# Inverting the 16x16 diagonal blocks of a head's triangular matrices on VectorE, gathered and scattered by DMA, with K and Q interleaved

## The reference, cut to what matters

```python
def step(state, inp):
    q_t, k_t, v_t, b_t, d_t = inp
    Sk = jnp.einsum('bhi,bhipj->bhpj', k_t, state)
    delta = (v_t - Sk) * b_t[..., None]
    upd = jnp.einsum('bhi,bhpj->bhipj', k_t, delta)
    state = state * d_t[:, :, None, :, None] + upd
    o = jnp.einsum('bhi,bhipj->bhpj', q_t, state)
    return (state, o)
```

## Time and profile before

| what | us |
|---|---|
| median of 3 runs | 1288.95 (1286.04 to 1291.09) |
| the profiled execution | 1287.92 |
| its span, first to last instruction | 1286.2 |
| PE busy | 1232.8 (96%) |
| DVE busy | 1069.8 (83%) |
| ACT busy | 912.1 (71%) |
| POOL busy | 910.0 (71%) |

### The profile page before, as it was taken

One profiled execution on the slowest core, in us unless ns is written; L12 is line 12 of the kernel. 1 busy time (PEld: TensorE's weight loads), 2 busy tenths in 40 slices (PEclk: granted clock), 3 DMA queues, 4 the chain that ended last, 5 costly groups with the idle time before them and its releaser, 6 DMA issues.

```text
span 1286.2 us, 33400 instructions
## 1 busy us (share of the span) xinstructions
PE 1232.8 (96%) x12362; PEld 1059.9 (82%) x12362; DVE 1069.8 (83%) x2393; ACT 912.1 (71%) x2536; POOL 910.0 (71%) x1184
## 2 busy tenths in 40 slices
PE   9899988989999999999999999999999999999997
PEld 7565445778989898889998989989999889999885
DVE  5797225999888999998997897889898879888788
ACT  4003553587888778787878787778878878778675
POOL 3122443667887868867876878788888888878765
PEclk9898989999999999999999999999999999999999
DMA  7931112222111011210112212121321213121221
GB/s 232 242 104 38 45 40 95 83 46 75 29 46 45 26 35 42 67 35 24 45 37 69 62 51 79 45 85 51 84 54 48 83 34 88 31 83 30 74 69 54
DMA packets 62773, 83.77 MB, mean 65 GB/s; under 512 B 8276, under 2 KB 46420, under 8 KB 62612
## 3 DMA queue, kind: packets, MB, share of 16 engines
q1 hardware_dynamic: 57876, 67.34, 18.8%
q0 software_dynamic: 4736, 14.29, 4.0%
HBM read 68.65 MB, written 12.77 MB: 63 GB/s over the span
## 4 chain that ended last, share of the span: by engine, by line
PE 71%; DVE 17%; DMA 4%; issue 4%; ACT 3%; POOL 2%; SPq 0%; DVEq 0%; POOLq 0%; ACTq 0%
PE ps L1225 19%; PE ps L1622 4%; PE ps L1575 4%; PE ps L1589 4%; PE ps L1559 3%; PE ps L1518 3%; PE ps L1531 3%; PE ps L1528 3%; PE ps L1560 3%; PE ps L1585 3%; DVE yv L2003 2%; PE ps L1630 2%; PE ps L1412 2%; PE ps L1498 2%; PE ps L1597 2%
## 5 line engine op out<-in xcount | busy, mean ns | idle before, releaser
L2385 ACT ACTIVATE XY<-ps 128x512 f16<-128x512 f32 x384 | 218.2, 601 | 87.8 <-PE ps L1531 85.8
L2116 DVE TENSOR_TENSOR ZL<-ps,cst 128x256 f16<-128x256 f32 x384 | 151.9, 417 | 16.0 <-PE ps L1518 14.7
L2003 DVE SCALAR_TENSOR_TENSOR yv<-ps,cw,yv 128x511 f32<-128x511 f32 (+2 forms) x192 | 142.6, 744 | 6.6 <-ACT yv L2329 4.1
L1225 PE MATMUL ps<-XH,WVh 128*128 128x256 f32 (+1 forms) x384 | 131.8, 343 | 2.1 <-DVE xt L2201 1.4
L1225 PE MATMUL ps<-XH,WVl 128*128 128x256 f32 (+1 forms) x384 | 122.4, 319 | 0.0
L1225 PE MATMUL ps<-XL,WVh 128*128 128x256 f32 (+1 forms) x384 | 122.3, 319 | 0.0
L1528 PE MATMUL ps<-ZL,XY 128*128 128x64 f16 x1536 | 103.8, 193 | 1.5 <-DVE ZL L2116 1.2
L1531 PE MATMUL ps<-XY,ZL 128*128 128x64 f16 x1536 | 103.4, 193 | 0.0
L1518 PE MATMUL ps<-XY,LT 128*128 128x64 f16 x1536 | 93.8, 193 | 3.9 <-ACT XY L2385 2.7
L2419 ACT ACTIVATE sq<-O 128x128 bf16<-128x128 f32 x256 | 79.7, 311 | 19.6 <-DVE O L2166 8.3
L1518 PEld LDWEIGHTS ps<-XY,LT 128*128 128x128 f16 x1536 | 74.9, 98 | 22.0 <-issue 11.5
(11 more groups left out here) (337 smaller groups left out, 4279.3 us busy)
## 6 DMA issues: line engine op xcount, KB each, us to landing
RC<-crow SPq DMA_DIRECT2D x128, 128.0 KB
WV<-in_WV SPq DMA_DIRECT2D x16, 512.0 KB, 3.7
exr<-in_ex SPq DMA_DIRECT2D x16, 384.0 KB, 3.5
WK<-in_WK SPq DMA_DIRECT2D x16, 256.0 KB, 3.0
WO<-in_WO SPq DMA_DIRECT2D x16, 256.0 KB, 2.7
rows_out<-st SPq DMA_DIRECT2D x7, 512.0 KB
KS<-spread SPq DMA_DIRECT2D x12, 256.0 KB, 8.7
QS<-spread SPq DMA_DIRECT2D x12, 256.0 KB, 12.5
```

What stands on the lines that cost most here:

```text
L1225: m = pe.matmul(o, a, b, start=c + k == 0, stop=c == 1 and k == 2)
L2003: m = dve.scalar_tensor_tensor(out=dst[:, k:512], in0=ps[:, bk, 0:512 - k], scalar=cw[:, h, j, 3 - k:4 - k], in1=dst[:, k:512], op0=ALU.mu ...
L2116: leave(dve.tensor_tensor(half(ZL[:, k - 2], k, 0), p, lv(k), ALU.mult), "a", u, k)
L2385: leave(act.activation(changed(u, k), ps[:, bank("b", u, k), :].rearrange("p (c n t) -> p c n t", c=2, t=1 << (k - 1)), ACT.Copy), "b", u, k)
```

## The change

The levels 1 to 4 of every inverse are no longer done by `x1`, `a` and `b` on PE, DVE and ACT; `LEVELS` becomes `range(5, 8)`. In their place the 16x16 diagonal blocks are inverted directly:

- `gram`, `pl`, `pm` of a chunk come earlier (`plan_chunk`, rank `4 * h - 6.3 + 0.6 * i`). The two 16-bit parts of L go by DMA (`ls`) to an array `parked` in DRAM, and PT goes to `decayed` (`ps`).
- When the 4 chunks of a head are parked, 8 DMAs (`dg`) gather its 128 diagonal blocks (16 matrices x 8 blocks) into LC, one block of 256 elements to a partition. The run that a packet moves is 16 elements of 2 bytes.
- 16 DVE instructions (`iv1`, `iv2`, `iv3`) invert the blocks by substitution on sizes 2, 4, 8 and 16; each waits for the one before, save for the second ones of pairs.
- ACT casts the result and its transpose (`xc`), and 16 DMAs (`sx`) scatter them into the zeroed diagonal form in `parked`, again in runs of 32 bytes.
- For each chunk one DMA (`ld`) brings X, Y, L and the low part back into XYLM, and one (`pd`) brings PT back.
- Two DMAs write zeros to `parked` among the small loads of layer 0.
- K and Q share a tile KQ, and `gram` is one matmul of 256 columns to each sequence in place of two of 128.
- POOL's `py` and `xi` go; `pl` and `pm` do the same cast, subtraction and diagonal in another order.
- The keys of a head come earlier (rank `4 * h - 8.5` in place of `4 * h - 6`), and `RANK` and `LATER` have other numbers throughout, so that the order within all queues differs.

```diff
-LEVELS = range(2, 8)
-C_IO = C_LV + 6 * 64
+C_ID, C_SEL, C_U, C_ONE, C_LV = 0, 128, 256, 384, 512
+LEVELS = range(5, 8)
...
-    P.add(("pt", u), rank + 0.1, ("DVE", 0.79, (("gram", u), "DVE"), earlier(4, "so", "PE", 0), earlier(4, "so", "PE", 1)),
-          gives=("gram", u))
-    P.add(("pl", u), rank + 0.1, ("POOL", 1.5, (("gram", u), "DVE"), earlier(3, "c", "DVE"), earlier(3, "r", "PE")))
-    P.add(("py", u), rank + 0.1, ("POOL", 1.2, (("pl", u), "POOL")))
-    P.add(("pm", u), rank + 0.2, ("POOL", 1.2, (("pl", u), "POOL")))
-    P.add(("xi", u), rank + 0.1, ("POOL", 0.48, earlier(3, "r", "PE"), (("cc", 1), "POOL")))
-    P.add(("x1", u), rank + 0.4, ("PE", 0.12, (("pl", u), "POOL"), (("cc", 1), "POOL")),
-          ("DVE", 0.34, earlier(3, "r", "PE"), (("xi", u), "POOL")), takes=True, gives=("x1", u))
-    last = ("x1", u), "DVE"
+    P.add(("pt", u), rank + 0.1, ("DVE", 0.79, (("gram", u), "DVE"), earlier(2, "ps", "SP")), gives=("gram", u))
+    P.add(("ps", u), rank + 0.2, ("SP", 1.0, (("pt", u), "DVE"), earlier(8, "pd", "SP")))
+    P.add(("pl", u), rank + 0.1, ("POOL", 0.6, (("gram", u), "DVE"), earlier(2, "ls", "SP")))
+    P.add(("pm", u), rank + 0.1, ("POOL", 2.1, (("pl", u), "POOL")))
+    P.add(("ls", u), rank + 0.2, ("SP", 1.0, (("pm", u), "POOL"), earlier(8, "ld", "SP")))
+
+
+def plan_blocks(P, h):
+    rank = 4 * h - 3.8
+    units = [(("ls", 4 * h + i), "SP") for i in range(4)]
+    P.add(("dg", h), rank, ("SP", 4.0, *units, (("iv1", h - 1), "DVE") if h else None))
+    P.add(("iv1", h), rank + 0.1, ("DVE", 2.5, (("dg", h), "SP"), (("xc", h - 1), "ACT") if h else None))
+    P.add(("iv2", h), rank + 0.1, ("DVE", 1.3, (("iv1", h), "DVE")))
+    P.add(("iv3", h), rank + 0.1, ("DVE", 1.3, (("iv2", h), "DVE")))
+    P.add(("xc", h), rank + 0.2, ("ACT", 0.9, (("iv3", h), "DVE"), (("sx", h - 1), "SP") if h else None))
+    P.add(("sx", h), rank + 0.2, ("SP", 8.0, (("xc", h), "ACT")))
...
+    P.add(("ld", u), rank - 0.5, ("SP", 1.5, (("sx", h), "SP"), earlier(3, "c", "DVE")))
+    P.add(("pd", u), rank + 0.5, ("SP", 1.0, (("ps", u), "SP"), earlier(2, "so", "PE", 0), earlier(2, "so", "PE", 1)))
+    last = ("ld", u), "SP"
...
+        parked = nc.dram_tensor("parked", (2, 4, 128, 16, 128), F16, kind="Internal").ap()
+        decayed = nc.dram_tensor("decayed", (8, 128, 512), F32, kind="Internal").ap()
...
+        KQ = sb("KQ", [128, 3, 2, 1024])
+        K, QC = KQ[:, :, 0, :], KQ[:, :, 1, :]
...
+                for k in range(2):
+                    sp.dma_start(parked[k, 0:2].rearrange("k p q t -> k p (q t)").bitcast(U16),
+                                 A["blank"].unsqueeze(0).broadcast_to((2, 128, 2048))).then_inc(d_l1, 16)
...
+                elif what == "ps":
+                    w.wait_ge(*done("gram", h))
+                    if h > 7:
+                        w.wait_ge(d_pd[h % 2], 16 * ((h - 8) // 2 + 1))
+                    sp.dma_start(decayed[h % 8], PTE[:, h % 2].rearrange("p l t -> p (l t)")).then_inc(d_ps[h % 2], 16)
+                elif what == "ls":
+                    w.wait_ge(s_one, nth("POOL", "pm", h))
+                    if h > 7:
+                        w.wait_ge(d_ld[(h - 8) % 3], 16 * ((h - 8) // 3 + 1))
+                    i = 4 * (h % 4)
+                    sp.dma_start(parked[h // 4 % 2, 2:4, :, i:i + 4, :].rearrange("k p q t -> p k (q t)"), LM[:, h % 2]
+                                 ).then_inc(d_ls[h % 2], 16)
+                elif what == "dg":
+                    for p in range(2):
+                        w.wait_ge(d_ls[p], 16 * (2 * h + 2))
+                    if h:
+                        w.wait_ge(s_iv, IV * (h - 1) + 1)
+                    for b in range(8):
+                        at = slice(16 * b, 16 * b + 16)
+                        sp.dma_start(LC[at].rearrange("q (j i) -> q j i", i=16),
+                                     parked[h % 2, 2, at, :, at].rearrange("j q i -> q j i")).then_inc(d_dg, 16)
+                elif what == "sx":
+                    w.wait_ge(d_l1, 96)
+                    w.wait_ge(s_xc, 2 * h + 2)
+                    for b in range(8):
+                        at = slice(16 * b, 16 * b + 16)
+                        for k in range(2):
+                            sp.dma_start(parked[h % 2, k, at, :, at].rearrange("r q c -> q r c"),
+                                         XY16[at, k, :].rearrange("q (r c) -> q r c", c=16)).then_inc(d_sx, 16)
+                elif what == "ld":
+                    w.wait_ge(d_sx, 256 * (h // 4 + 1))
+                    if h > 2:
+                        w.wait_ge(*done("c", h - 3))
+                    i = 4 * (h % 4)
+                    sp.dma_start(XYLM[:, h % 3], parked[h // 4 % 2, :, :, i:i + 4, :].rearrange("k p q t -> p k (q t)")
+                                 ).then_inc(d_ld[h % 3], 16)
+                elif what == "pd":
+                    w.wait_ge(d_ps[h % 2], 16 * (h // 2 + 1))
+                    if h > 1:
+                        for b in range(2):
+                            w.wait_ge(*full("so", h - 2, b))
+                    sp.dma_start(PT[:, h % 2].rearrange("p l t -> p (l t)"), decayed[h % 8]).then_inc(d_pd[h % 2], 16)
...
-                        kt = K[:, h % 3, 128 * n:128 * n + 128]
-                        pe.matmul(ps[:, bk, 256 * b:256 * b + 128], kt, kt, start=True, stop=True)
-                        m = pe.matmul(ps[:, bk, 256 * b + 128:256 * b + 256], kt,
-                                      QC[:, h % 3, 128 * n:128 * n + 128], start=True, stop=True)
-                    signal(m, *x)
-                elif what == "x1":
-                    u = x[1]
-                    bk = enter(*x)
-                    w.wait_ge(s_const, 2)
-                    w.wait_ge(s_lt, nth("POOL", "pl", u))
-                    for l in range(4):
-                        m = pe.matmul(ps[:, bk, 64 * l:64 * l + 64], LT[:, u % 3, l, :], half(id16[:], 1, 0), start=True, stop=True)
+                        at = slice(128 * n, 128 * n + 128)
+                        m = pe.matmul(ps[:, bk, 256 * b:256 * b + 256].rearrange("p (k t) -> p k t", k=2),
+                                      K[:, h % 3, at], KQ[:, h % 3, :, at], start=True, stop=True)
...
+            def times_left(wd, o, to):
+
+                left = part_of(XC, 17 * o + 16 * wd, (16, wd), (0, wd), (1, wd))
+                upper = part_of(XC, 17 * o, (0, wd), (1, wd), (16, wd))
+                dve.tensor_tensor(to.rearrange("p (r c k) -> p r c k", r=wd, c=wd), left, upper, ALU.mult).then_inc(s_iv, 1)
...
+            def inner_blocks(n):
+
+                xc = XC[:].rearrange("p (r c) -> p r c", r=16)
+                dve.tensor_scalar(xc, LC[:].rearrange("p (c r) -> p r c", r=16), -1.0, None, ALU.mult).then_inc(s_iv, 1)
...
+                for k in range(2):
+                    times_left(4, 8 * k, PR[:, 64 * k:64 * k + 64])
+                w.wait_ge(s_iv, n + 8)
+                dve.tensor_reduce(ZC[:, 16:48], PR[:, 0:128].rearrange("p (a k) -> p a k", k=4), AX.X, ALU.add).then_inc(s_iv, 1)
+                w.wait_ge(s_iv, n + 9)
+                for k in range(2):
+                    times_right(4, 8 * k, 16 + 16 * k, PR[:, 64 * k:64 * k + 64])
+                w.wait_ge(s_iv, n + 11)
+                dve.tensor_reduce(part_of(XC, 64, (136, 2), (16, 4), (1, 4)),
+                                  PR[:, 0:128].rearrange("p (n r c k) -> p n r c k", n=2, r=4, c=4), AX.X, ALU.add).then_inc(s_iv, 1)
...
+                elif what == "iv2":
+                    h = x[1]
+                    w.wait_ge(s_iv, IV * h + 12)
+                    times_left(8, 0, PR[:])
+                    w.wait_ge(s_iv, IV * h + 13)
+                    dve.tensor_reduce(ZC[:, 0:64], PR[:].rearrange("p (a k) -> p a k", k=8), AX.X, ALU.add).then_inc(s_iv, 1)
...
+                elif what == "xc":
+                    h = x[1]
+                    w.wait_ge(s_iv, IV * (h + 1))
+                    if h:
+                        w.wait_ge(d_sx, 256 * h)
+                    act.activation(XY16[:, 0, :], XC[:], ACT.Copy).then_inc(s_xc, 1)
+                    act.activation(XY16[:, 1, :].rearrange("p (c r) -> p c r", c=16), XC[:].rearrange("p (r c) -> p c r", r=16),
...
-                    pool.tensor_copy(MH[:, u % 2], M[:, u % 2]).then_inc(s_mh, 1)
-                    w.wait_ge(s_mh, nth("POOL", *x))
-                    pool.affine_select(out=LT[:, u % 3], in_=MH[:, u % 2], compare_op=ALU.not_equal, fill=1.0, base=0,
-                                       pattern=[[0, 4], [1, 128]], channel_multiplier=-1).then_inc(s_lt, 1)
-                elif x[0] == "xi":
-                    u = x[1]
-                    w.wait_ge(s_const, 2)
-                    if u > 2:
-                        w.wait_ge(*full("r", u - 3))
-                    pool.tensor_copy(half(xy(u, 0), 1, 1), half(spread4(id16[:]), 1, 1)).then_inc(s_xi, 1)
-                elif x[0] == "py":
```

(36 more changed lines are left out.)

366 lines of the change are left out of this document (182 added, 184 removed), and 30 rows, old and new, of tables (LATER, RANK).

## The result

The change makes the kernel slower: 1352.1 us median (1347.7 to 1364.1, 4 runs) against 1289.2 for the kernel before in the same session, a ratio of 1.051 [1.045, 1.057]. I had forecast 1232 us.

What follows compares the result with a forecast made beforehand. It took PE as the bound with DVE 10 points behind, and DVE filling to 97.8% after the change. 250 + 960.8 + 4.8 + 15 = 1230.6 us, plus 1.7 around the span: 1232 us; range 1195 to 1305.

Steps and rivals of the forecast that it cites:

- rival of a free DVE: Rival: DVE is no second bound, PE sets the pace at 98.7% busy, time 1202 us; chance 0.22.
- the start: Before the first state step: the first inverse waits for four chunks, 28 us late, 15 us lost, bounds 0 and 35.
- PE's savings: PE from 250 us on: 76.8 us of matmuls and 13 of changes of kind go, 1007.5 falls to 917.7 us.
- The length: From 250 us on: DVE fills to 97.8%, so its 939.7 us of work take 960.8 us.
- The zeroing: Zeroing of `parked` among the expert loads of layer 0: costs 0, at most 5 us.
- SP issues 40 more DMAs to a head: SP's queue: 17 us of a head's 60 go to added issues, counted as nothing.
- the rival on SP's queue: Rival: SP's queue stands behind `ld`, holding row loads; gain gone at 3.5 us a head, 6 give 1328; chance 0.12.
- The inversion's own length: Block inversion on DVE: 8.1 us a head, 130 us for 16 heads, bounds 5.3 and 14.7 a head.
- the DMA share: DMA engines over the whole kernel: 553 of 980 us, 56%, so no DMA bound was counted.
- the interleave: K and Q interleaved in `gram`: gives nothing, 8 x 0.11 us before and 4 x 0.215 after.
- DVE's work: DVE from 250 us on: 914.2 falls to 809.7 us, the inversion adds 130, giving 939.7 us.
- the one of DVE as sole bound: Rival: DVE operations wait for POOL, equal to before at 11.5 us a head, 1340 us at 14.7; chance 0.10.

Runs made afterwards that it cites:

- f3: e1 in the same order without gathers, scatters and their waits, and without 14 of the inversion's 16 DVE instructions a head: 1247.5 us, 0.969.
- f1: e1 in the same order with 14 of the inversion's 16 DVE instructions a head left out, all DMAs kept: 1277.6 us, 0.993.
- e1: The changed kernel with the two zeroing DMAs having the 128 partitions as outer dimension in place of the 2 planes: 1319.4 us, 1.023.
- f2: e1 in the same order without gathers, scatters and the waits on them, the inversion kept on a block of zeros: 1298.1 us, 1.007.
- f8: e1 in the same order with the whole inversion done twice on DVE, 32 instructions a head in place of 16: 1448.2 us, 1.125.
- h4: The kernel before, own order, with the inversion's 16 DVE instructions added unused, spread in four parts over a head's four chunks: 1405.1 us, 1.092.
- f4: e1 in the same order with one gather of eight and one scatter of sixteen a head, all waits kept: 1295.8 us, 1.006.
- e4: The kernel before without levels 2 to 4, with the inversion's 16 DVE instructions a head added on zeros, no DMAs added: 1432.9 us, 1.114.
- h3: The kernel before, own order, with the inversion's 16 DVE instructions added unused in one block behind each head's first P: 1440.2 us, 1.119.
- h2: e1 in the same order with the ten small instructions of iv1 left out, cast, sign, iv2 and iv3 kept: 1286.1 us, 0.999.

## Why the prediction was wrong

The difference splits along four kernels. The last three steps differ in one thing each; the first holds all the rest of the change. The forecast can be split at the same places: its rival of a free DVE, 1202 us, is the change with nothing to pay for the inversion, and the forecast is 30 us above that.

| step, us | forecast | measured |
|---|---|---|
| levels gone, other order, late start (before 1289.1, f3 1247.5) | -87 | -41.6 |
| gathers and scatters (f3 to f1) | 0 | +30.1 |
| inversion on DVE, 14 of its 16 instructions (f1 to e1) | +30 | +41.8 |
| zeroing (e1 to after, 1352.1) | 0 | +32.7 |

The order of the steps matters: by f2 in place of f1 it is 50.6 for the inversion and 21.3 for gathers and scatters. Of the 120 us that were missing, 45 are in the first row, 30 in the second, 12 in the third and 33 in the last. What makes up the 45 is seen in part, in the start and PE's savings below; its cause stays open.

- **The length, "If DVE fills up to the 97.8% of its densest stretch": 960.8 us.** This is the term that failed most. From 250 us on e1 takes 1073.2 us, where the sum has 980.6 with its ends and start. I took a fill from 120 us and let it hold for 960, and counted no DMA work beside it. Neither engine filled: e1 shows PE at 89.9% and DVE at 88.7% from 300 to 1200 us, and even f3, with neither inversion nor chain, 95.4% and 85.3%. Nor does another share make a rule: DVE showed 89.8% in f8 and 90.5% in h4, but 91.7% in f4 and 93.3% in e4 over the same stretch. 939.7 divided by 0.90 would give 1315.6 us, near e1's 1319; but I know the 0.90 only from the result, and e1 also pays for its DMAs, so that match is luck. The 12% that DVE had free in the kernel before were no reserve: h3 shows that work put into it lengthens the kernel by more than itself. In the changed kernel, which has lost some 104 us of DVE's work, the first 54 us put back cost 0.16 each (f1 to h2), the next 36 nearly their length.
- **The zeroing, "0, at most 5 us".** 32.7 us. I priced its bytes at the mean rate of the queue and didn't look at the dimension by which they are shared out.
- **"SP issues 40 more DMAs to a head ... I count nothing".** The issues cost 16 us and the short packets about 7, the landings nothing that shows: by place the rival on SP's queue, by size 1.5 us a head where I had put the deciding point at 3.5. Its wording, a queue behind `ld`, wasn't tested alone.
- **The start, 15 us of 28.** In e1, which has no stall in layer 0, the first W starts at 347.9, 40.7 us later than before. PE is busy 112.4 us from 250 to 400 where it was 145.4, so up to 33 us are lost, near the upper bound of 35. In f3, without gathers and scatters, it still starts at 342.9: two of the four landings I had summed and the 24 issues are gone and 5 us came back, so they aren't what delays it. What in the order does isn't isolated.
- **PE's savings.** In f3 the time from first to last W falls by 75.3 us, but its first W is 36 us late, and all in all 41.6 us are won: PE's relief is real and worth less than its size. PE's busy time from 250 us on falls from 1007.5 to 937.7 us in f3 and to 958 in e1, not to the 918 forecast. Part of it may be the clock, whose mean was 0.985 before, 0.961 in f3 and 0.953 in e1.
- **The inversion's own length (8.1 us, measured 7.5, in e1 7.3), the DMA share and the interleave** were right. DVE's work (939.7; 942.5 from 250 us on in e1) was right in part by luck: the inversion took 13 us less than the 130 and the rest of DVE 16 more than the 809.7. Products stretched from 677 to 1218 and 1417 ns and sums stayed at 686, as the earlier trace rows had let expect. But more than the ten products were exposed: the sign of 16 elements, with one SBUF input, took 336 ns where the earlier trace rows has 167, and the cast 571 for 284.

Of the rivals, the one of DVE as sole bound had the right place and the wrong condition: it needed no inversion of 11.5 us. The measured 1352 lies outside the range of 1195 to 1305, and e1, 1319, does too. No experiment gave a version with the reference's output that beats the kernel before; e1 is the best with the whole change in it.

## What to carry to other kernels

The idle share of an engine with a fixed queue, in a kernel that is tuned tightly around it, is no safe room for new work: price work that comes on top of what the engine did before at its full length, above all where the profile shows another engine at 98% only because its partners are never late, and test that price by adding the instructions to the old kernel before building the change. Work that only takes the place of removed work can be far cheaper, as the first step of the dose shows. Count DMA issues as time of the queue that issues them, and read the first dimension of each pattern, also of a transfer that is only there to set something up, and who waits on its semaphore.
